# Masked matrix kept row by row and stored in four transfers by batch, with work of the first and last passes placed elsewhere

## What is computed

```python
# layer 1, C = 128, on the layer-normed x
q, k, v = x @ Wq + bq, x @ Wk + bk, x @ Wv + bv
k = k / norm(k)
alpha, beta, gate = sigmoid(x @ Wa + ba), sigmoid(x @ Wb + bb), sigmoid(x @ Wg + bg)
for t in range(2048):                       # state S is 128 x 128 for each batch
    S = S @ (alpha_t * (I - beta_t * k_t k_t^T)) + beta_t * v_t k_t^T
    o_t = (q_t @ S) * gate_t
x = x + o @ Wo + bo
# layer 2, on the layer-normed x: rms norms, then 1024 slots
logits = rms(x, gamma_x) @ rms(slot_embeds, gamma_slot)^T
slots = softmax(logits, over positions)^T @ rms(x, gamma_x)
x = x + softmax(logits, over slots) @ (gelu(slots @ w1) @ w2)
```

## Time and profile before

| | us |
|---|---|
| three runs | 1190.31, 1190.20, 1187.94 |
| the profiled execution, its own time | 1187.25 |
| span of its trace | 1185.4 |
| VectorE busy in the span | 938.2 |
| GpSimd busy in the span | 314.5 |
| ScalarE busy in the span | 735.6 |

### The profile page before, as it was taken

One profiled execution on the slowest core, in us unless ns is written; L12 is line 12 of the kernel. 1 busy time (PEld: TensorE's weight loads), 2 busy tenths in 40 slices (PEclk: granted clock), 3 DMA queues, 4 the chain that ended last, 5 costly groups with the idle time before them and its releaser, 6 DMA issues.

```text
span 1185.4 us, 26905 instructions
## 1 busy us (share of the span) xinstructions
PE 1113.2 (94%) x8600; PEld 854.5 (72%) x8600; DVE 938.2 (79%) x2195; ACT 735.6 (62%) x1385; POOL 314.5 (27%) x389
## 2 busy tenths in 40 slices
PE   4489999999999889899999999999999999999998
PEld 2378888888888764587786486787486787487787
DVE  4789888888889747997586898576898666998665
ACT  3446567665766445687663697664587664497763
POOL 3647656676567611000021000022000022000012
PEclk9699999999999989999999999999999999999999
DMA  6113432233233343232273031264031355000155
GB/s 191 45 45 81 125 98 85 87 107 119 80 88 95 99 96 100 66 72 57 55 170 78 2 72 45 63 147 103 2 72 32 74 123 130 0 1 1 22 119 128
DMA packets 185519, 94.02 MB, mean 79 GB/s; under 512 B 123680, under 2 KB 176928, under 8 KB 185440
## 3 DMA queue, kind: packets, MB, share of 16 engines
q1 hardware_dynamic: 178384, 75.40, 26.6%
q0 software_dynamic: 5792, 17.05, 4.9%
q10 hardware_dynamic: 1264, 0.53, 0.2%
HBM read 38.42 MB, written 29.36 MB: 57 GB/s over the span
## 4 chain that ended last, share of the span: by engine, by line
PE 66%; DVE 16%; issue 11%; ACT 4%; POOL 2%; DMA 1%; DVEq 1%; SPq 0%; ACTq 0%; POOLq 0%
PE m_wide L2015 14%; PE m_wide L1992 7%; PE m_wide L1978 7%; PE m_wide L1898 6%; PE a_bank L1095 4%; DVE m_Dm L1598 3%; PE a_bank L1107 3%; PE a_bank L1157 2%; DVE m_El L1606 2%; PE m_wide L2003 2%; ACT m_Eh L1781 2%; PE a_bank L1233 2%; PE a_bank L1146 2%; DVE cmax L1569 2%; PE m_wide L1952 2%
## 5 line engine op out<-in xcount | busy, mean ns | idle before, releaser
L1536 POOL DMA_DIRECT2D out_dram<-m_o x64 | 35.4, 553 | 627.1 <-DVE m_o L1720 514.3
L1952 PE MATMUL m_wide<-m_X,m_Eh 128*128 128x257 f16 (+1 forms) x1024 | 171.5, 273 | 2.7 <-DVE m_El L1606 2.7
L1898 PE MATMUL m_wide<-seT,XT 128*128 128x512 f16 x672 | 147.3, 379 | 0.9 <-issue 0.8
L2015 PE MATMUL m_wide<-m_Ph,m_Th 128*128 128x257 f16 x512 | 140.4, 274 | 4.3 <-DVE m_Pl L1645 4.3
L1952 PE MATMUL m_wide<-m_X,m_El 128*128 128x257 f16 (+1 forms) x512 | 139.7, 273 | 0.0
L2015 PE MATMUL m_wide<-m_Ph,m_Tl 128*128 128x257 f16 x512 | 139.4, 272 | 0.0
L2015 PE MATMUL m_wide<-m_Pl,m_Th 128*128 128x257 f16 x512 | 139.1, 272 | 0.0
L1898 PEld LDWEIGHTS m_wide<-seT,XT 128*128 (+1 forms) x672 | 65.5, 98 | 78.5 <-ACT L L1754 1.5
L1952 PEld LDWEIGHTS m_wide<-m_X,m_Eh 128*128 128x128 f16 x1024 | 99.2, 98 | 20.8 <-DVE m_El L1606 3.8
L1754 ACT COPY L<-m_wide 128x512 f32<-128x512 f32 (+1 forms) x112 | 65.1, 584 | 78.6 <-PE m_wide L1898 77.8
L1774 ACT ACTIVATE m_E<-m_Dm,m_eshift 128x512 f32<-128x512 f32 x128 | 92.5, 722 | 23.5 <-DVE m_Dm L1598 22.5
(11 more groups left out here) (198 smaller groups left out, 2712.5 us busy)
## 6 DMA issues: line engine op xcount, KB each, us to landing
L<-in_L_attn_x_dram SPq DMA_DIRECT2D x16, 512.0 KB, 7.2
Mrep<-M_dram SPq DMA_DIRECT2D x32, 256.0 KB
x_dram<-x SPq DMA_DIRECT2D x16, 512.0 KB, 6.6
m_X<-X_dram SPq DMA_DIRECT2D x128, 64.0 KB, 1.8
m_x1t<-x_dram POOLq DMA_DIRECT2D x32, 256.0 KB, 3.5
out_dram<-m_o POOLq DMA_DIRECT2D x64, 128.0 KB, 2.4
M_dram<-M_ SPq DMA_DIRECT2D x16, 256.0 KB, 2.6
X_dram<-Xh SPq DMA_DIRECT2D x16, 256.0 KB, 2.3
```

What stands on the lines that cost most here:

```text
L1898: last = pe.matmul(lg[t % 4], XT[:, sx * KD + k, bass.ds((4 * g + t) * P, P)], seT[:, ss, k, z * HS:(z + 1) * HS], start=(c == 0), stop=(c ...
L1952: last = pe.matmul(acc[v][q], e[t % 4][:, qs], X[:, sx, bass.ds(4 * g + t, 1), 0:XW].rearrange("q a n -> q (a n)"), start=first and e is E ...
L2015: last = pe.matmul(co[p], a, pp[:, e, 0:XW], start=(c == 0), stop=(c == 3 * NS - 1))
```

## The change

- `M[q]` is laid out as (partition, batch, 128 columns). `blocks_out` issues four transfers, one for each batch, with runs of 64 bytes; all waits on `M_out` count 64 for a block where they counted 16.
- GpSimd has no `half_cut`. TensorE's third `products` reads the quarter in `M` itself and waits for `M_ok`.
- The low part of `w2` (was `mixture_weights(4)`, one VectorE instruction) is made by GpSimd at the end of its `step(-3)`, in two instructions over 128 x 2048.
- VectorE's `mixture_weights(3)` moves behind the decays of the same `step(-2)`.
- `slots_scaled` (eight instructions) is split, four at the end of `step(-1)` and four at the end of `step(0)`; `slots_high` goes to the end of `step(1)`, `slots_low` to that of `step(12)`. VectorE's loop starts two passes later.
- In `step(-2)` GpSimd does the key norms first and `spread_beta` right after the residual; TensorE turns the keys and multiplies them ahead of `turn_Z`, ScalarE copies accordingly.
- `early_maxima` of tiles 0 and 1 go into `step(14)`, those of tiles 2 to 5 into `step(15)`; before, tiles 0 to 2 stood in `step(15)`.

```diff
-        M = two("M", [P, NBK, B, BS])
-        Mhalf = two("Mhalf", [HP, B, HP])
+        M = two("M", [P, B, P])
...
             def blocks_out(c, q):
                 sp.wait_ge(M_ok, c + 1)
-                sp.dma_start(M_dram[0:NBK * P * B * BS].rearrange("(e p f) -> p e f", e=NBK, p=P),
-                             M[q][:, :, :, :].rearrange("p e b t -> p e (b t)")).then_inc(M_out, 16)
+                columns = M_dram[0:NBK * P * B * BS].rearrange("(e p b t) -> p e b t", e=NBK, p=P, b=B)
+                for b in range(B):
+                    sp.dma_start(columns[:, :, b, :], M[q][:, b, :].rearrange("p (e t) -> p e t", t=BS))\
+                        .then_inc(M_out, 16)
...
-                out, used = value(sp, 16 * (c + 1)), value(sp, c)
+                out, used = value(sp, 16 * B * (c + 1)), value(sp, c)
...
-                    half_cut(i + 2, q)
...
                 if at == -3:
+                    second_weights_low()
                     slot_norms()
+
+            def second_weights_low():
+                pool.wait_ge(w2h_ok, 1)
+                pool.tensor_scalar(w2_in, w2_in, WSCALE, None, ALU.mult).then_inc(w2h_ok, 1)
+                pool.wait_ge(w2h_ok, 2)
+                pool.tensor_tensor(w2s[:, 1, :, :], w2_in, w2s[:, 0, :, :], ALU.subtract).then_inc(w2h_ok, 1)
...
-                    mixture_weights(3)
-                    mixture_weights(4)
-                if at == -1:
-                    slots_scaled()
-                    slots_high()
                 for s in range(BS - 1):
...
+                        if at == NCH - 2:
+                            early_maxima(0)
...
+                        if at == NCH - 2:
+                            early_maxima(1)
...
                 if at == -3:
                     mixture_weights(2)
+                if at == -2:
+                    mixture_weights(3)
...
                 if at == -1:
+                    slots_scaled(0, NS // 2)
+                if at == 0:
+                    slots_scaled(NS // 2, NS)
+                if at == 1:
+                    slots_high()
+                if at == NCH - 4:
                     slots_low()
                 if at == NCH - 1:
-                    for t in range(3):
+                    for t in range(2, 6):
                         early_maxima(t)
...
-            steps(dve, step)
-            for t in range(3, NT):
+            steps(dve, step, first=1)
+            for t in range(6, NT):
                 early_maxima(t)
...
-                pe.wait_ge(moff_ok, made)
+                pe.wait_ge(moff_ok if n < NCUT else M_ok, made)
...
-                        last = pe.matmul(bank[4][HP:, bs], Mhalf[q][:, b, :], ZT[0:HP, bs], start=True, stop=True)
+                        last = pe.matmul(bank[4][HP:, bs], M[q][0:HP, b, HP:], ZT[0:HP, bs], start=True, stop=True)
```

More of the change, by code:

```diff
@@ L447, in cut @@
                 at = C_MASK + n * P
[L448 to L451, removed]
+                pool.tensor_tensor(moff[q][:, n], M[q][:, :, :], over_batches(const[:, at:at + P]), ALU.mult)\
                     .then_inc(moff_ok, 1)
[L454 to L459, removed]
             def spread_blocks(c, q):
@@ L480, in step @@
                 at = i if isinstance(i, int) else None
+                if at == -2:
+                    if live(i + 3):
+                        key_norms(i + 3)
                 if live(i + 2):
                     residual(i + 2, q)
+                if at == -2:
+                    if live(i + 3):
+                        spread_beta(i + 3)
                 if live(i + 2):
@@ L490, in step @@
                     cut(i + 2, q, 0)
-                    half_cut(i + 2, q)
                 if live(i):
                     output_norm(i)
-                if live(i + 3):
+                if live(i + 3) and at != -2:
                     key_norms(i + 3)
@@ L579, in system @@
                 if later(c, 2):
[L580 to L584, removed]
+                    dve.wait_ge(moff_ok, NCUT * (c - 1))
+                    dve.wait_ge(M_out, 16 * B * (c - 1))
+                dve.tensor_tensor(M[q][:, :, :], by_batch[6], gamb[q][:, :, :], ALU.mult).then_inc(M_ok, 1)
             def product(c, s):
@@ L703, in mixture_weights @@
                     dve.tensor_copy(w1s[:, 0, :, :], w1_g).then_inc(w1_ok, 1)
[L704 to L707, removed]
                 elif step == 5:
@@ L710, in mixture_weights, with slots_scaled @@
                     dve.tensor_tensor(w1s[:, 1, :, :], w1_g, w1s[:, 0, :, :], ALU.subtract).then_inc(w1_ok, 1)
[L712 to L717, removed]
+            def slots_scaled(first, past):
+                if first == 0:
+                    dve.wait_ge(srn_ok, 1)
+                    dve.wait_ge(w2h_ok, 3)
+                    dve.wait_ge(w1_ok, 3)
+                    dve.wait_ge(gxs_ok, 1)
+                for e in range(first, past):
                     last = dve.scalar_tensor_tensor(slots_g[:, e, :], slots_in[:, e, :], srn[:, e:e + 1], gxs[:, :],
                                                     ALU.mult, ALU.mult)
-                last.then_inc(slots_ok, 1)
+                if past == NS:
+                    last.then_inc(slots_ok, 1)
             def slots_high():
@@ L1016, in step @@
                     gates(i + 3, r)
+                if at == -2:
+                    if live(i + 3):
+                        turned_keys(i + 3)
                 if live(i + 2):
@@ L1149, in products @@
             def products(c, q, n):
-                turned, made = value(pe, NLV * c + n + 1), value(pe, NLV * c + (NCUT - n if n < NCUT else NLV))
+                turned, made = value(pe, NLV * c + n + 1), value(pe, NCUT * c + NCUT - n if n < NCUT else c + 1)
                 pe.wait_ge(pool_consts, 1)
                 pe.wait_ge(ZT_ok, turned)
-                pe.wait_ge(moff_ok, made)
+                pe.wait_ge(moff_ok if n < NCUT else M_ok, made)
                 for b in range(B):
@@ L1276, in step @@
                     spread_alpha(i + 3)
+                if at == -2:
+                    if live(i + 3):
+                        turn_keys(i + 3, r)
+                if at == -2:
+                    if live(i + 3):
+                        system(i + 3)
                 if live(i + 2):
```

## The result

The changed kernel took 1197.13 us (median of five runs, 1192.4 to 1199.97), the kernel before beside it 1189.64 (1186.71 to 1190.31): a ratio of 1.0066, 95% interval 1.0038 to 1.0095, 4.5 to 11.3 us slower. The profiled execution took 1198.67 with a span of 1197.1. The forecast of 1193.8 has the sign and half the size. The spread is itself about twice that of before. All ratios here are of undisturbed executions: one of e10's eleven, of 3995 us, is left out of its ratio.

What follows compares the result with a forecast made beforehand. TensorE was taken to bound the loop, VectorE close behind. Terms summed to +3.6 us on the profiled 1187.25, giving 1190.9; with the median of the runs 2.95 above that execution, 1193.8 was forecast, range 1182 to 1208.

Steps and rivals of the forecast that it cites:

- The four transfers and the quarter: M's store and the dropped GpSimd copy: loads 2.1 us later at 13.1 ns a run, within the slack, 0 us.
- Step -2: VectorE freed of the low part of w2, columns and M of block 1 come earlier: -3.2 us.
- Start of step -1: Slot instructions no longer ahead of the columns, -4.4 us, and no clock fall after TensorE's wait, -1.6 us.
- End of step -1: Four slot scalings there, three each waiting for a GpSimd instruction, in place of one 2.27 us instruction: +2.6 us.
- step 0: Four more scalings alternating with GpSimd's queue and delaying Xl, +4.6 us, plus a clock fall, +1.6 us.
- step 1: High part of the slots at its end, then Xl blocked by a GpSimd cut: +2.2 us.
- step 12: Low part of the slots and a blocked instruction, +3.5 us; one clock fall for steps -1 and 12, +1.6 us.
- the clock: TensorE falling to 1.2 GHz after long waits: +1.6 us in step 0, +1.6 once for steps -1 and 12.
- Tail: Maxima of two tiles and a memset moved into a VectorE wait of 6.18 us in step 14: -3.3 us.
- the alternation that does not come: Rival: slot scalings pass GpSimd's queue at 0.4 us each, no clock fall; -8.7 us, 1181.5, chance 0.25.
- The loop bound by `M`: Rival: M's longer way to the column loads bounds each loop pass; 10 to 18 us more, about 1208, chance 0.28.
- The late head: Rival: GpSimd's w2 instructions run long, key norms come late, step -2 gains 0; 1197.0 us, chance 0.09.

Runs made afterwards that it cites:

- e10: Kernel before, block layout and 256-byte runs kept, with the store of M cut into four transfers: 1190.16 us, ratio 1.0001.
- e2: Changed kernel with the slot instructions back where they were before the change: 1181.39 us, ratio 0.9948 to the kernel before.
- e1: Kernel before with only the row layout of M, its four transfers and the quarter read from M: 1190.1 us, ratio 1.0011.
- e6: Kernel before with only the edits of step -2: 1187.38 us, ratio 0.9983.
- e9: Changed kernel with TensorE repeating work ahead of its waits in steps -1 and 12: 1195.23 us, ratio 1.0043 to the kernel before.
- e7: Kernel before with only VectorE's steps 0 and 1 written out instead of one turn of its loop: 1185.88 us, ratio 0.9975.
- e5: Kernel of e1 with the store's runs halved to 32 bytes, eight transfers: 1233.92 us, ratio 1.0396 to the kernel before.

## Why the forecast had the sign and half the size

The single parts add up: 1.3 (layout) - 2.0 (step -2) - 2.5 (tail) - 3.0 (written out) = -6.2 us, each to within 1.1 to 1.4, and e2, which has them all, measured -6.2. The moved slots make up the rest, 14.0, where the prediction's terms for them come to -4.4 - 1.6 + 2.6 + 6.2 + 2.2 + 5.1 = +10.1. The changed kernel's profiled execution took longer than its median and e2's less than its own: their spans differ by 18.3 us, so the differences between these two traces below are some 4 us too large in all. By the prediction's steps:

*The four transfers and the quarter, 0*: right within what can be told (+1.3, interval -0.1 to +2.7). The loads go 1.9 us later, 2.1 forecast. The price of a run was too high: where e1's store is under way, the DMA engines are busy 0.91 at 102 GB/s,

```profile
263.50:264.50 1.00, 0.93 (x9) 0.72 (x7) 1.00 (x2) 0.59 (x3) 1.00 (x2) 1.00 0.91 102
```

that is 1.59 runs per ns over 16 engines, so 9.1 ns of an engine each and not 13.1. An estimate by the rule quoted from the Trainium skill, "DMA: Bandwidth & Descriptors", section "Why small descriptors are slow (HBM only)", was 9.0, and this trace agrees. What made the way nearly as long all the same lies elsewhere. The issues come 0.6 us apart (SP's 0.37 us was the price of one alone, four take 2.28), and the engines move the store over some 2.6 us where it was 1.3. From its last bytes to the issue of the loads about 1 us passes, where it was 0.4; why is open.

*Step -2, -3.2*: -2.0 (-3.1 to -0.8). The step itself gained more than forecast: from `M` of block 0 to `M` of block 1 it takes 25.7 to 28.0 us in the eight traces with these edits and 29.7 to 32.6 in the six without. Times from the span's start mislead here, since `M` of block 0 alone comes anywhere from 26.5 to 30.3 us. Counted from it the columns began after 9.8 us, not the 9.1 forecast, and it is `M` coming without its wait that gained. GpSimd's two instructions took 9.5 us in all, within the bounds. What was missed is that step -1 up to its first column was not VectorE's alone, and gave part back: in e6 and e2, from `M` of block 1 to `M` of block 2, it takes 33.7 us, in the traces without the edits 29.7 to 30.8.

*Start of step -1, -4.4 and -1.6*: right. Between e2 (slots ahead of the columns) and the changed kernel the first column of block 1 moves from 72.04 to 67.59, 4.45 us. e2's stretch at 1.2 GHz around its wait of 3.87 is not in the other, and from `M` of block 1 to `M` of block 2 it takes 33.76 us in e2 and 27.85 in the changed kernel, 5.9 where 6.0 was forecast. e2's stretch:

```profile
74.00:81.00 7.00, 5.00 (x18) 3.54 (x19) 5.25 (x25) 2.07 (x10) 1.26 (x2) 0.51 0.00 0
```

*End of step -1, +2.6; step 0, +6.2; step 1, +2.2; step 12, +3.5 and +1.6*: here is the error. The instructions were priced well: 4.70 us (4.8 forecast), 5.77 and 1.21 (6.0 and 1.2), `Xl` blocked in steps 1 and 12 at 2.3. The term that failed is the clock. From `M` to `M` against e2, step -1 costs 5.2 us (29.88 against 24.65), step 0 8.9 (33.44 against 24.50), step 1 3.2 and the pass behind it 0.7, step 12 with what follows 5.9: 24 us in all, of which the slot instructions and `Xl` take 13. That leaves 11 us (some 7 if the 4 us above are taken off), where I counted 1.6 us of clock twice, from the window of 4 us behind one wait. The falls last 7, 14, 4 and 17 us. At 1.2 GHz TensorE is slow enough to make VectorE wait in turn, 1.82 us in step -1 and 1.94 in step 0. e9 puts the fall in step -1 at about 3 us, which is all that step costs beyond its instructions; that the rest in steps 0, 1 and 12 is the clock's too was not tested step by step. "I take one" for steps -1 and 12 was the wrong choice: the clock fell in step -1, which I may have counted, and in step 1, which I had not. In step 12 it falls for 7 us before the change as well, and 10 to 14 us in other kernels without slots there (e1, e7), so only part of the 17 us is the change's.

*Tail, -3.3*: -2.5 (-3.8 to -1.2), right in size, but not by the wait that I named: the maxima went into the wait of 3.68 us behind the weights, not into that of 6.18 ahead of them.

*Not in the sum, -3.0*: the loop of VectorE written out. I took the diff's `first=1` for a means to place the slots and gave it no price.

Of the rivals, the alternation that does not come would have needed scalings of 0.4 us; they took 1.2 to 1.4. The loop bound by `M` did not come; e5 shows it 0.4 us away. The late head did not come. Two errors of opposite sign, the clock and the written-out steps, hid each other in part, so that the forecast came as near as it did is partly luck.

## What to carry to other kernels

When setup instructions are moved off a path, look not only for room on their own engine but, on VectorE, for a moment in which GpSimd has no queue: the same eight scalings took 1.2 to 1.4 us each in one place of a step and 0.4 in another, and with the high and the low part moved along it made 15 us over the kernel. Measure the old place too: it was as good as the free one. Price a new wait of TensorE with what the clock does afterwards, over the whole stretch until it rises, and with the waits which slow TensorE then gives to the others. Measure a change of this kind in parts: four small edits that gained 6.2 us together were buried under one that lost 14.

## What the runs showed that I had not expected

Writing out two steps of one engine's loop, with no instruction changed, made the kernel 3.0 us faster (e7), in its trace all of it in the dispatches, behind 490 us. GpSimd took 5.39 us to scale 128x2048 values and 4.07 to subtract as many: the form with one input was the dearer. A store of 32-byte runs (e5) held the loop up by 2.9 us in a pass though it moves the same bytes as one which does not wait at all. And TensorE, made to repeat transposes that nobody needs, kept its clock in step -1, and the step took 3 us less (e9). The kernel before runs at 1.2 GHz for 7 us in step 12 behind waits of at most 0.55 us.
